# Layer 1's attention: queries and keys rounded ahead of the exponentials, and VectorE's slot put in another order

## The chip, the core and the metric

The kernel runs on one core of a Trainium2 chip. The metric is the device time of one execution in microseconds; several runs are taken and their median is given.

## What is computed

Two blocks of a gated cross-attention network on x of shape (8, 128, 512), each with a gated attention and a gated feed-forward part, all in float32:

```python
x = x + tanh(g_xattn[0]) * _L0_xattn_ref(_layernorm(x), ctx_4096, mask, ...)
x = x + tanh(g_ffn[0])   * _L0_ffn_ref(_layernorm(x), ...)
x = x + tanh(g_xattn[1]) * _L1_xattn_ref(_layernorm(x), ctx_4096, ...)
x = x + tanh(g_ffn[1])   * _L1_ffn_ref(_layernorm(x), ...)
```

The change concerns the third line. With 32 query heads that share 8 key/value heads, 128 queries a batch, and 256 keys (128 of the context, 128 of x itself):

```python
kv = concatenate([context, latents], axis=1)
q, k, v = latents @ Wq, kv @ Wk, kv @ Wv          # by head, 128 wide
q, k = rms_norm(q, q_norm_w), rms_norm(k, k_norm_w)
probs = softmax(q @ k.T / sqrt(128))
return (probs @ v, by head) @ Wo
```

## The kernel before, in words

There is no scheduler: each engine has its own instruction list, written by hand, and semaphores hold the lists together. The time up to about 940 us goes to layer 0 (keys and values of the context, attention, feed-forward). From there on layer 1's attention runs in 64 **slots**, the functions `slot1` of every engine. A slot is one key/value head and one batch; `BODY` = 8 slots (the batches) are a **turn**, and 8 turns are the heads. The first turn and the last are written out, those between are a loop.

Full precision is had from three passes of matmuls: every operand is split into a high part (the value rounded, by ScalarE, names in `_hi`) and a low part (what the rounding left, by VectorE, names in `_lo`), and `passes` multiplies high by high, high by low and low by high.

The work is pipelined over slots. In slot i, with count i + 1 as the current pair:

- **TensorE** (L2530 and on): keys and values of pair i + 2 (`keys_values`), transposes of q (L2547) and of k (L2552) for pair i + 1, the output projection of pair i - 2 (waits for `ot1_lo_done`), the queries of pair i + 2, the scores of pair i + 1 (wait for `qt1_lo_done`, `kt1_lo_done` and the earlier exponentials), and last the attention output of pair i - 1 (waits for `pt1_lo_done`).
- **ScalarE** (L1250 to L1285): `kv_out` (v_hi and the squares of k, L1213 and L1214), the four exponentials `exponentials1(i)` (L1235), qt_hi (L1263) and kt_hi (L1265), pt_hi (L1244, waits for the DMA that brings the transposed probabilities), in five slots a turn a piece of the next head's weights (`split_hi`, L1203), q_out (q_sb and q_sq, L1220 and L1221), and ot_hi (L1250, waits for the attention output).
- **VectorE** (L1974 to L2026): k_mean (k_ms, L1901), two reciprocals of the exponentials' sums (`inverse_sums1`, L1948), qt_lo (L1985), kt_lo (L1987), v_low (two v_lo, L1906), k_scaled (L1913, twice: the context's keys from SBUF, then x's own from a PSUM bank; its tile lies in `fbias`, and the rows call it so), `split_lo` (w_lo, L1896, in slots 1 to 5 of every turn but the last), accumulate1 (the residual, L1952), probabilities_lo (pt_lo, L1957), probabilities_in_blocks (two halves of 32x32 transposes, L1966), q_mean (q_ss and q_ms, L1920 and L1922), maxima1 (two nmax, L1938, and nb, L1943), output1_lo (ot_lo, L1971).
- **GpSimd**: k_root, `normalised(i)` (the probabilities times the reciprocals, two halves, L764, each behind its reciprocal), q_root (L630).
- **SP's queue**: the context's keys and values, the weights' pieces, and the round trip of the probabilities: a store to DRAM when both halves of blocks are made (L592), then four loads that bring them back transposed (L595) for pt_hi of the next slot.

The exponentials read the scores' banks, so the next scores wait for them; they wait for nb (`shift1_done`) and for the transposes of the pair before (`blocks1_done`), since these read the same tile p1.

Of the kernel before, what the change touches and what calls it, by code (L numbers as in the profile page):

```python
# [39 lines left out]
U = 64  # L40
# [17 lines left out]
def build(nc, x, ctx_t, mask, gates, wk0, wv0, wq0, w0, bias0, lnw, qweight, lut4, lut8, ffn0_bias, w1, qk_norm, ffn1_w, ffn1_bias, out):  # L58
    stack = ExitStack()
    with stack:  # L60
# [153 lines left out]
        sum1 = tmp("sum1", [P, 4], fp32)  # L214
        rn1 = tmp("rn1", [P, 4], fp32)
# [590 lines left out]
        def _(act):  # L806
# [424 lines left out]
            def exponentials1(count, parity):  # L1231
                act.wait_ge(shift1_done, count)
                wait(act, blocks1_done, 2 * (count - 1))
                for a in range(4):
                    last_op = nc.scalar.activation(p1[:, a, :], by2((S0B, S1B)[a // 2][:, :])[:, a % 2, :], ACT.Exp,  # L1235
                                                   bias=nb1[:, a:a + 1], scale=q_r[:, parity, a:a + 1],
                                                   accum_out=sum1[:, a:a + 1])
                    if a % 2:
                        last_op.then_inc(exp1_done, 1)
# [12 lines left out]
            def slot1(t, j):  # L1252
                i = BODY * t + j
                first = isinstance(t, int) and t == 0
                last = isinstance(t, int) and t == TL - 1

                if not (last and j == BODY - 1):
                    wait(act, o1_ps, i - 2)
                    kv_out(i + 2, (j + 1) % 4, 4 * t + (j + 1) // 2 + 1)
                if not (first and j == 0):  # L1260
                    exponentials1(i, (j - 1) % 2)
                act.wait_ge(qt1_ps, i + 1)
                nc.scalar.activation(qt_hi[:, :], QTB[:, :], ACT.Copy).then_inc(qt1_hi_done, 1)  # L1263
                act.wait_ge(kt1_ps, i + 1)
                nc.scalar.activation(kt_hi[:, :], KTB[:, 0:256], ACT.Copy, scale=kw[:, 0:1]).then_inc(kt1_hi_done, 1)  # L1265
                if first and j == 1:
                    transposed_hi(2, 6)
                    transposed_hi(2, 7)
# [47 lines left out]
        def _(dve):  # L1316
# [627 lines left out]

            def inverse_sums1(count):
                for half_p in (0, 2):
                    dve.wait_ge(exp1_done, 2 * count - 1 + half_p // 2)
                    nc.vector.reciprocal(rn1[:, half_p:half_p + 2], sum1[:, half_p:half_p + 2]).then_inc(recip1_done, 1)  # L1948

# [24 lines left out]
            def slot1(t, j):  # L1974
# [5 lines left out]
                if ahead:  # L1980
                    k_mean(i + 2)
                if lag1:
                    inverse_sums1(i)
                dve.wait_ge(qt1_hi_done, i + 1)
# [3 lines left out]
                                               in1=kt_hi[:, :].bitcast(fp32), op0=ALU.mult,  # L1988
                                               op1=ALU.subtract).then_inc(kt1_lo_done, 1)
                if ahead:  # L1990
                    v_low(i + 2, (j + 1) % 4)
                    k_scaled(i + 2, (j + 1) % 4)
                if not last and 1 <= j < 6:
                    split_lo(t + 1, j - 1, (t + 1) % 2)
                if not (first and j < 3):
                    accumulate1(i - 2, (j - 3) % B)
                if not (first and j < 2):
                    probabilities_lo(i - 1, (j - 1) % 2)
                if not (first and j < 1):
                    probabilities_in_blocks(i)  # L2000
                if last and j in (4, 6):
# [17 lines left out]
                if ahead:  # L2019
                    q_mean(i + 2)  # L2020
                maxima1(i + 1, j % 2)
                if first and j == 0:
                    transposed_lo(2, 4)
                    transposed_lo(2, 5)
                if not (first and j < 2):
                    output1_lo(i - 1)  # L2026
            for j in range(BODY):
                slot1(0, j)
# [7 lines left out]
            last_gate = tg[:, 3:4]  # L2036
            inverse_sums1(U)
            feed_forward(3, last_gate, 0)
# [627 lines left out]
```

## Time and profile before

| | |
|---|---|
| median of 3 runs | 1704.34 us (1704.33 to 1705.15) |
| the profiled execution | 1706.54 us |
| its span, first to last instruction | 1704.7 us |
| busy: TensorE matmuls / weight loads | 1643.4 (96%) / 1436.2 (84%) |
| busy: VectorE / ScalarE / GpSimd | 1230.3 (72%) / 1022.6 (60%) / 589.8 (35%) |
| granted TensorE clock, mean | 0.994 |
| layer 1's attention | from about 940 to 1690 us |

Busy shares are means over stages with different limits. To see what a slot waits for, the timeline of one slot is read engine by engine: a row gives the start and the duration of an instruction, and in brackets how long its engine stood idle before it and what ended that. Records of one engine overlap a little at their ends, so the distance of two starts is what an instruction costs its followers.

### The profile page before, as it was taken

What the parts mean: (1) busy time and instruction counts of PE and PEld (TensorE: products, weight loads), DVE (VectorE), ACT (ScalarE), POOL (GpSimd) and SP (SyncE); (2) the same over time, 40 slices, a digit from 0 to 9 for tenths busy, and PEclk for the clock granted to TensorE, in tenths of its full rate; (3) what the DMA queues carried; (4) which work ended last, traced back from release to release, by engine and by line L of the source; (5) the groups of instructions that cost most, each with busy time, mean ns of one, the idle gap of its engine ahead of it and who ended that gap; (6) DMA issues with size and microseconds to landing.
All of it is one profiled execution on the core that took longest, in us unless ns stands there. A gap on an engine that the chain in (4) does not pass through costs nothing.

```text
span 1704.7 us, 30549 instructions
## 1 busy us (share of the span) xinstructions
PE 1643.4 (96%) x9757; PEld 1436.2 (84%) x9757; DVE 1230.3 (72%) x2274; ACT 1022.6 (60%) x2511; POOL 589.8 (35%) x584
## 2 busy tenths in 40 slices
PE   9999999999999999999999799999999999999987
PEld 8899999999988888888888678888888888888875
DVE  6444437676787777877778677878787878777775
ACT  5344443345867677677766566666666666666652
POOL 3422223211334444444335333333333333333332
PEclk9999999999999999999999899999999999999999
DMA  6444444535233333333332243434343434343322
GB/s 231 171 166 148 148 171 157 191 133 182 72 106 102 120 98 111 113 95 126 98 106 82 72 136 122 148 119 146 118 159 123 145 123 148 123 148 111 115 93 97
DMA packets 126671, 220.43 MB, mean 129 GB/s; under 512 B 11664, under 2 KB 96016, under 8 KB 123024
## 3 DMA queue, kind: packets, MB, share of 16 engines
q1 hardware_dynamic: 126608, 219.63, 38.6%
q8 instruction: 35, 0.57, 0.1%
q14 instruction: 28, 0.23, 0.0%
HBM read 141.99 MB, written 77.59 MB: 129 GB/s over the span
## 4 chain that ended last, share of the span: by engine, by line
PE 58%; DVE 20%; ACT 9%; DMA 6%; issue 5%; SPq 1%; POOL 1%; DVEq 0%; ACTq 0%; POOLq 0%
PE bank L2134 20%; PE bank L2079 8%; PE bank L2080 8%; PE bank L2081 8%; PE bank L2311 6%; ACT p L1235 4%; DMA probabilities_transposed<-blocks_of_probabilities 2%; DMA blocks_of_probabilities<-probabilities_in_blocks 2%; DVE pt_lo L1957 2%; PE bank L2269 2%; PE bank L2347 2%; DVE probabilities_in_blocks L1966 2%; PE bank L2431 2%; DVE w_lo L1896 2%; DVE wl L1575 1%
## 5 line engine op out<-in xcount | busy, mean ns | idle before, releaser
L630 POOL TENSOR_TENSOR q_r<-q_ms,half 128x4 f32<-128x4 f32 x64 | 64.4, 1007 | 378.5 <-DVE q_ms L1922 378.5
L2079 PE MATMUL bank<-w_hi,xt_hi 128*128 (+2 forms) x512 | 173.4, 339 | 0.1
L2080 PE MATMUL bank<-w_lo,xt_hi 128*128 (+2 forms) x512 | 173.2, 338 | 0.0
L2081 PE MATMUL bank<-w_hi,xt_lo 128*128 (+2 forms) x512 | 172.0, 336 | 0.0
L711 POOL TENSOR_TENSOR pr<-pr,rn 128x512 f32<-128x512 f32 x64 | 67.5, 1055 | 291.4 <-DVE rn L1600 291.4
L1235 ACT ACTIVATE p<-bank,nb,q_r 128x256 f32<-128x256 f32 x256 | 141.4, 576 | 7.4 <-DVE nb L1943 7.4
L764 POOL TENSOR_TENSOR p<-p,rn 128x512 f32<-128x512 f32 x128 | 133.1, 1041 | 28.7 <-DVE rn L1948 25.2
L1244 ACT ACTIVATE pt_hi<-probabilities_transposed 128x1024 fp32r<-128x1024 f32 x64 | 68.0, 1063 | 94.6 <-DMA probabilities_transposed<-blocks_of_probabilities 94.6
L1075 ACT ACTIVATE pr<-sc,nmax 128x128 f32<-128x128 f32 x256 | 99.9, 391 | 40.0 <-DVE nmax L1585 39.6
L2079 PE MATMUL bank<-w_hi,ot_hi 128*128 (+1 forms) x256 | 107.3, 419 | 16.7 <-DVE ot_lo L1971 15.8
L2079 PE MATMUL bank<-w0o_hi,ot_hi 128*128 128x512 f32 x256 | 105.4, 412 | 5.0 <-DVE residual L1592 4.5
L1250 ACT ACTIVATE ot_hi<-bank 128x512 fp32r<-128x512 f32 x64 | 38.3, 598 | 119.2 <-PE bank L2081 119.2
L2079 PEld LDWEIGHTS bank<-w_hi,xt_hi 128*128 128x128 f32 x512 | 97.0, 189 | 13.9 <-POOL w_lo L728 0.3
L2080 PEld LDWEIGHTS bank<-w_lo,xt_hi 128*128 128x128 f32 x512 | 97.1, 190 | 12.0
L2081 PEld LDWEIGHTS bank<-w_hi,xt_lo 128*128 128x128 f32 x512 | 96.8, 189 | 10.9
L2134 PE MATMUL bank<-vw_hi,t_hi 128*128 128x256 f32 x368 | 104.1, 283 | 0.6 <-DVE vw_lo L1364 0.6
L2134 PE MATMUL bank<-vw_hi,t_lo 128*128 128x256 f32 x368 | 104.1, 283 | 0.0
L2134 PE MATMUL bank<-vw_lo,t_hi 128*128 128x256 f32 x368 | 104.1, 283 | 0.0
L1948 DVE RECIPROCAL rn<-sum 128x2 f32<-128x2 f32 x128 | 21.2, 166 | 110.9 <-ACT p L1235 110.9
L2080 PE MATMUL bank<-w_lo,ot_hi 128*128 (+1 forms) x256 | 101.1, 395 | 0.0
L2081 PE MATMUL bank<-w_hi,ot_lo 128*128 (+1 forms) x256 | 100.8, 394 | 0.0
L2081 PE MATMUL bank<-w0o_hi,ot_lo 128*128 128x512 f32 x256 | 100.1, 391 | 0.0
(292 smaller groups left out, 5574.6 us busy)
## 6 DMA issues: line engine op xcount, KB each, us to landing
blocks_of_probabilities<-probabilities_in_blocks SPq DMA_DIRECT2D x64, 512.0 KB, 2.7
probabilities_transposed<-blocks_of_probabilities SPq DMA_DIRECT2D x256, 128.0 KB, 2.8
stage<-w SPq DMA_DIRECT2D x35, 512.0 KB, 3.3
keys_of_layer<-kout SPq DMA_DIRECT2D x16, 1024.0 KB, 4.8
values_of_layer<-vout SPq DMA_DIRECT2D x16, 1024.0 KB, 5.2
kt<-keys_of_layer SPq DMA_DIRECT2D x64, 256.0 KB, 3.3
vs<-values_of_layer SPq DMA_DIRECT2D x64, 256.0 KB, 2.8
vraw<-wv SPq DMA_DIRECT2D x10, 1024.0 KB, 6.7
```

The source lines that it names most:

```text
L630: pool.tensor_tensor(dst, src, exponent, ALU.pow).then_inc(done, 1)
L711: pool.tensor_tensor(by4(pr), by4(pr), rn[:, :].unsqueeze(2).to_broadcast([P, 4, P]), ALU.mult).then_inc(norm_done, 1)
L764: pool.tensor_tensor(p1[:, half_p:half_p + 2, :], p1[:, half_p:half_p + 2, :], rn1[:, half_p:half_p + 2].unsqueeze(2).to_broadcast([P, 2, ...
L1075: last_op = nc.scalar.activation(by4(pr)[:, a, :], by4(sc)[:, a, :], ACT.Exp, bias=nmax[:, a:a + 1], accum_out=ssum[:, a:a + 1])
L1235: last_op = nc.scalar.activation(p1[:, a, :], by2((S0B, S1B)[a // 2][:, :])[:, a % 2, :], ACT.Exp, bias=nb1[:, a:a + 1], scale=q_r[:, pari ...
L1244: nc.scalar.activation(pt_hi[:, :, :].rearrange("p kc (qb n) -> p kc qb n", qb=4), by_key_block(ptr1[:, parity, :]), ACT.Copy).then_inc(pt ...
L1250: nc.scalar.activation(by_head(ot1_hi[:, :]), by_query_block(O1B[:, :]), ACT.Copy).then_inc(ot1_hi_done, 1)
L2079: nc.tensor.matmul(out_ap, l_hi, r_hi, start=(c == 0), stop=False)
L2080: nc.tensor.matmul(out_ap, l_hi, r_lo, start=False, stop=False)
L2081: op = nc.tensor.matmul(out_ap, l_lo, r_hi, start=False, stop=(c == n - 1))
L2134: op = nc.tensor.matmul(out_ap, l, r, start=start, stop=False, skip_group_check=True)
L2311: op = nc.tensor.matmul(bank[which][:, :], l[:, a, c, :], r[:, c, :], start=start, stop=False, skip_group_check=True)
```

## The change

On ScalarE, qt_hi and kt_hi move ahead of the exponentials. On VectorE the slot is reordered: the reciprocals, once together ahead of qt_lo, are taken apart; w_lo moves from behind k_scaled to between kt_lo and the first reciprocal; v_low stands between the two reciprocals and k_scaled behind the second; the transposes (probabilities_in_blocks) move ahead of pt_lo; and ot_lo moves ahead of the maxima. No instruction is added or removed; TensorE's, GpSimd's and SP's lists stay as they are.

```diff
--- before.py
+++ after.py
@@ -1257,12 +1257,12 @@
                 if not (last and j == BODY - 1):
                     wait(act, o1_ps, i - 2)
                     kv_out(i + 2, (j + 1) % 4, 4 * t + (j + 1) // 2 + 1)
-                if not (first and j == 0):
-                    exponentials1(i, (j - 1) % 2)
                 act.wait_ge(qt1_ps, i + 1)
                 nc.scalar.activation(qt_hi[:, :], QTB[:, :], ACT.Copy).then_inc(qt1_hi_done, 1)
                 act.wait_ge(kt1_ps, i + 1)
                 nc.scalar.activation(kt_hi[:, :], KTB[:, 0:256], ACT.Copy, scale=kw[:, 0:1]).then_inc(kt1_hi_done, 1)
+                if not (first and j == 0):
+                    exponentials1(i, (j - 1) % 2)
                 if first and j == 1:
                     transposed_hi(2, 6)
                     transposed_hi(2, 7)
@@ -1942,10 +1942,9 @@
                 dve.wait_ge(q1_root_done, count)
                 nc.vector.tensor_tensor(nb1[:, :], nmax1[:, :], q_r[:, parity, :], ALU.mult).then_inc(shift1_done, 1)
 
-            def inverse_sums1(count):
-                for half_p in (0, 2):
-                    dve.wait_ge(exp1_done, 2 * count - 1 + half_p // 2)
-                    nc.vector.reciprocal(rn1[:, half_p:half_p + 2], sum1[:, half_p:half_p + 2]).then_inc(recip1_done, 1)
+            def inverse_sums1(count, half_p):
+                dve.wait_ge(exp1_done, 2 * count - 1 + half_p // 2)
+                nc.vector.reciprocal(rn1[:, half_p:half_p + 2], sum1[:, half_p:half_p + 2]).then_inc(recip1_done, 1)
 
             def accumulate1(count, b):
                 dve.wait_ge(y1_ps, count)
@@ -1979,25 +1978,28 @@
                 ahead = not (last and j == BODY - 1)
                 if ahead:
                     k_mean(i + 2)
-                if lag1:
-                    inverse_sums1(i)
                 dve.wait_ge(qt1_hi_done, i + 1)
                 nc.vector.tensor_tensor(qt_lo[:, :], QTB[:, :], qt_hi[:, :].bitcast(fp32), ALU.subtract).then_inc(qt1_lo_done, 1)
                 dve.wait_ge(kt1_hi_done, i + 1)
                 nc.vector.scalar_tensor_tensor(out=kt_lo[:, :], in0=KTB[:, 0:256], scalar=kw[:, 0:1],
                                                in1=kt_hi[:, :].bitcast(fp32), op0=ALU.mult,
                                                op1=ALU.subtract).then_inc(kt1_lo_done, 1)
+                if not last and 1 <= j < 6:
+                    split_lo(t + 1, j - 1, (t + 1) % 2)
+                if lag1:
+                    inverse_sums1(i, 0)
                 if ahead:
                     v_low(i + 2, (j + 1) % 4)
+                if lag1:
+                    inverse_sums1(i, 2)
+                if ahead:
                     k_scaled(i + 2, (j + 1) % 4)
-                if not last and 1 <= j < 6:
-                    split_lo(t + 1, j - 1, (t + 1) % 2)
                 if not (first and j < 3):
                     accumulate1(i - 2, (j - 3) % B)
+                if lag1:
+                    probabilities_in_blocks(i)
                 if not (first and j < 2):
                     probabilities_lo(i - 1, (j - 1) % 2)
-                if not (first and j < 1):
-                    probabilities_in_blocks(i)
                 if last and j in (4, 6):
 
                     dve.wait_ge(acc1_done, i - 2)
@@ -2018,12 +2020,12 @@
                     transposed_lo(2, 7)
                 if ahead:
                     q_mean(i + 2)
+                if not (first and j < 2):
+                    output1_lo(i - 1)
                 maxima1(i + 1, j % 2)
                 if first and j == 0:
                     transposed_lo(2, 4)
                     transposed_lo(2, 5)
-                if not (first and j < 2):
-                    output1_lo(i - 1)
             for j in range(BODY):
                 slot1(0, j)
             with dve.Fori(1, TL - 1) as t:
@@ -2034,7 +2036,8 @@
 
 
             last_gate = tg[:, 3:4]
-            inverse_sums1(U)
+            inverse_sums1(U, 0)
+            inverse_sums1(U, 2)
             feed_forward(3, last_gate, 0)
             transposed_lo(3, 1)
             probabilities_in_blocks(U)
```

ScalarE, a slot without a weight's piece (the names: p is the exponentials' output). Before:

```order
L1214 ACTIVATE fbias,k_ss<-bank 128x128
L1235 ACTIVATE p,sum<-bank,nb,q_r 128x256 x4
L1263 ACTIVATE qt_hi<-bank 128x512
L1265 ACTIVATE kt_hi<-bank,kw 128x256
L1244 ACTIVATE pt_hi<-probabilities_transposed 128x1024
L1220 ACTIVATE q_sb<-bank 128x512
```

Now:

```order
L1214 ACTIVATE fbias,k_ss<-bank 128x128
L1261 ACTIVATE qt_hi<-bank 128x512
L1263 ACTIVATE kt_hi<-bank,kw 128x256
L1235 ACTIVATE p,sum<-bank,nb,q_r 128x256 x4
L1244 ACTIVATE pt_hi<-probabilities_transposed 128x1024
L1220 ACTIVATE q_sb<-bank 128x512
```

qt_hi and kt_hi have passed the four exponentials; pt_hi follows these directly.

VectorE, one slot of the first turn with a weight's piece, from the ot_lo that closes the slot before to pt_lo (fbias is k_scaled's tile). Before:

```order
L1971 TENSOR_TENSOR ot_lo<-bank,ot_hi 128x512
L1901 TENSOR_SCALAR k_ms<-k_ss 128x2
L1948 RECIPROCAL rn<-sum 128x2 x2
L1985 TENSOR_TENSOR qt_lo<-bank,qt_hi 128x512
L1987 SCALAR_TENSOR_TENSOR kt_lo<-bank,kw,kt_hi 128x256
L1906 TENSOR_TENSOR v_lo<-keys_values_of_context,v_hi 128x128
L1906 TENSOR_TENSOR v_lo<-bank,v_hi 128x128
L1913 TENSOR_SCALAR fbias<-keys_values_of_context,k_r 128x128
L1913 TENSOR_SCALAR fbias<-bank,k_r 128x128
L1896 TENSOR_TENSOR w_lo<-stage,w_hi 128x1024
L1952 SCALAR_TENSOR_TENSOR residual<-bank,tg,residual 128x512
L1957 TENSOR_TENSOR pt_lo<-probabilities_transposed,pt_hi 128x1024
```

Now, the same stretch from its ot_lo to the first k_scaled:

```order
L1970 TENSOR_TENSOR ot_lo<-bank,ot_hi 128x512
L1938 TENSOR_REDUCE nmax<-bank 128x2 x2
L1943 TENSOR_TENSOR nb<-nmax,q_r 128x4
L1901 TENSOR_SCALAR k_ms<-k_ss 128x2
L1982 TENSOR_TENSOR qt_lo<-bank,qt_hi 128x512
L1984 SCALAR_TENSOR_TENSOR kt_lo<-bank,kw,kt_hi 128x256
L1896 TENSOR_TENSOR w_lo<-stage,w_hi 128x1024
L1947 RECIPROCAL rn<-sum 128x2
L1906 TENSOR_TENSOR v_lo<-keys_values_of_context,v_hi 128x128
L1906 TENSOR_TENSOR v_lo<-bank,v_hi 128x128
L1947 RECIPROCAL rn<-sum 128x2
L1913 TENSOR_SCALAR fbias<-keys_values_of_context,k_r 128x128
```

Before, both reciprocals stand ahead of qt_lo, and w_lo behind k_scaled; the maxima and nb are ahead of this ot_lo, outside the rows. Now the maxima and nb follow ot_lo, w_lo stands ahead of the first reciprocal, v_lo behind the first and k_scaled behind the second. The end of the slot, now:

```order
L1913 TENSOR_SCALAR fbias<-bank,k_r 128x128
L1951 SCALAR_TENSOR_TENSOR residual<-bank,tg,residual 128x512
L1965 STREAM_TRANSPOSE probabilities_in_blocks<-p 128x2x2x4x32 x2
L1956 TENSOR_TENSOR pt_lo<-probabilities_transposed,pt_hi 128x1024
L1920 TENSOR_REDUCE q_ss<-q_sq 128x4
```

The transposes stand ahead of pt_lo, and behind q_ss and q_ms the next ot_lo follows directly.

## Rows read from the trace of the kernel before

**Rows 1.** Waits, TensorE's weight loads, 1010 to 1650 us: total us, times, longest.
```profile
PEld bank L2079 <- DVE ot_lo L1971: 19.5, 38, 2.1
PEld bank L2079 <- DVE pt_lo L1957: 12.8, 34, 1.5
```

**Rows 2.** Timeline, ScalarE, 1326 to 1339 us: start, duration, engine, line, operation [idle before].
```profile
1326.80 0.60 ACT L1250 ACTIVATE ot_hi<-bank 128x512 fp32r<-128x512 f32 x1 [2.54 <-PE bank L2081]
...
1328.64 0.57 ACT L1235 ACTIVATE p<-bank,nb,q_r 128x256 f32<-128x256 f32 x1
...
1330.81 0.62 ACT L1263 ACTIVATE qt_hi<-bank 128x512 fp32r<-128x512 f32 x1
1331.28 0.51 ACT L1265 ACTIVATE kt_hi<-bank,kw 128x256 fp32r<-128x256 f32 x1
...
1338.07 0.60 ACT L1250 ACTIVATE ot_hi<-bank 128x512 fp32r<-128x512 f32 x1 [1.70 <-PE bank L2081]
```

**Rows 3.** Timeline, ScalarE, 1371 to 1405 us.
```profile
1371.86 0.60 ACT L1250 ACTIVATE ot_hi<-bank 128x512 fp32r<-128x512 f32 x1 [2.12 <-PE bank L2081]
...
1404.26 0.60 ACT L1250 ACTIVATE ot_hi<-bank 128x512 fp32r<-128x512 f32 x1 [1.50 <-PE bank L2081]
```

**Rows 4.** Timeline, VectorE, 1326 to 1339 us.
```profile
1326.95 1.29 DVE L1938 TENSOR_REDUCE nmax<-bank 128x2 f32<-128x512 f32 x2
1328.28 0.16 DVE L1943 TENSOR_TENSOR nb<-nmax,q_r 128x4 f32<-128x4 f32 x1
1328.36 0.68 DVE L1971 TENSOR_TENSOR ot_lo<-bank,ot_hi 128x512 fp32r<-128x512 f32 x1
...
1329.88 0.17 DVE L1948 RECIPROCAL rn<-sum 128x2 f32<-128x2 f32 x1 [0.76 <-ACT p L1235]
...
1331.46 0.69 DVE L1985 TENSOR_TENSOR qt_lo<-bank,qt_hi 128x512 fp32r<-128x512 f32 x1 [0.32 <-ACT qt_hi L1263]
1332.07 0.47 DVE L1987 SCALAR_TENSOR_TENSOR kt_lo<-bank,kw,kt_hi 128x256 fp32r<-128x256 f32 x1
...
1332.86 0.28 DVE L1913 TENSOR_SCALAR fbias<-keys_values_of_context,k_r 128x128 f32<-128x128 f32 x1
...
1333.32 1.22 DVE L1896 TENSOR_TENSOR w_lo<-stage,w_hi 128x1024 f32 x1
1334.45 0.75 DVE L1952 SCALAR_TENSOR_TENSOR residual<-bank,tg,residual 128x512 f32<-128x512 f32 x1
1335.11 1.22 DVE L1957 TENSOR_TENSOR pt_lo<-probabilities_transposed,pt_hi 128x1024 fp32r<-128x1024 f32 x1
1336.24 1.30 DVE L1966 STREAM_TRANSPOSE probabilities_in_blocks<-p 128x512 f32<-128x512 f32 x2
1337.46 0.64 DVE L1920 TENSOR_REDUCE q_ss<-q_sq 128x4 f32<-128x512 f32 x1
```

**Rows 5.** Timeline, GpSimd, 1329 to 1333 us.
```profile
1330.12 2.13 POOL L764 TENSOR_TENSOR p<-p,rn 128x512 f32<-128x512 f32 x2 [0.23 <-DVE rn L1948]
```

**Rows 6.** Timeline, VectorE and GpSimd side by side, at 499 and 933 us.
```profile
499.53 1.87 DVE L1616 TENSOR_TENSOR w0o_lo<-stage0o,w0o_hi 128x1024 fp32r<-128x1024 f32 x1
...
499.14 1.17 POOL L689 TENSOR_TENSOR bm<-bias_sb,negm 128x512 f32<-128x512 f32 x1
500.27 1.71 POOL L659 TENSOR_TENSOR qraw<-qraw 128x256 f32<-128x256 f32 x1
...
933.70 4.77 POOL L728 TENSOR_TENSOR w_lo<-plain,w_hi 128x1024 fp32r<-128x1024 f32 x2
...
936.76 1.73 DVE L1337 TENSOR_SCALAR base_b<-mv 128x2 f32<-128x2 f32 x1
```

**Rows 7.** Timeline, VectorE and ScalarE, three late waits of layer 1.
```profile
1001.47 1.23 DVE L1957 TENSOR_TENSOR pt_lo<-probabilities_transposed,pt_hi 128x1024 fp32r<-128x1024 f32 x1 [1.47 <-ACT pt_hi L1244]
...
1591.10 1.23 DVE L1957 TENSOR_TENSOR pt_lo<-probabilities_transposed,pt_hi 128x1024 fp32r<-128x1024 f32 x1 [2.16 <-ACT pt_hi L1244]
...
1629.83 0.56 ACT L1235 ACTIVATE p<-bank,nb,q_r 128x256 f32<-128x256 f32 x1 [1.26 <-DVE nb L1943]
```

## The prediction

> **What bounds the kernel now.** I read the waits of TensorE first, then the rhythm of one ScalarE instruction, then one slot instruction by instruction on VectorE and ScalarE, and last GpSimd beside VectorE. The change touches layer 1's attention alone: 64 slots, eight to a turn, and only there TensorE's order meets VectorE's. In [rows 1] the weight loads of TensorE stand idle 19.5 us for ot_lo (the low part of the attention output, wanted by the output projection) and 12.8 us for pt_lo (the low part of the transposed probabilities, wanted by the attention output). Some 30 us is thus all that a better order could win.
>
> The rhythm is the start of ot_hi on ScalarE, once a slot. From 1326.80 to 1338.07 [rows 2] is 11.27 us, and the three slots from there to 1371.86 [rows 3] take 11.26 each: these are slots in which VectorE also makes a weight's low part, w_lo. Those without it, 1371.86 to 1404.26 [rows 3], take 32.40 for three, 10.80 each. Per turn five slots have w_lo (35 in all, the last turn has none) and three have not (21 in turns 0 to 6).
>
> Why 11.27: a loop closes on itself in every slot. ot_hi starts at 0 (1326.80), the exponentials at 1.84, qt_hi at 4.01, kt_hi at 4.48 [rows 2]; VectorE then runs without a gap qt_lo, kt_lo, the v and k operations, w_lo, the residual, pt_lo [rows 4]; pt_lo releases the attention output, and that the next ot_hi. pt_lo starts at 1335.11 and ot_hi at 1338.07, so **pt_lo to ot_hi is 2.96**. The 2.17 us of exponentials ahead of qt_hi lie in this loop, and VectorE mostly waits under them (the reciprocal of 1329.88 was 0.76 us idle before, [rows 4]). TensorE and VectorE are both nearly full, the loop is what is too long.
>
> **The change, part by part.** Steps on VectorE are distances of starts in [rows 4]: nmax to nb 1.33, nb to ot_lo 0.08 (I take 0.08 for each tiny operation: nb, k_ms, a reciprocal), qt_lo to kt_lo 0.61 (ot_lo, of the same shape, taken as 0.60), kt_lo 0.39 (its 0.47 less the overlap of 0.08 that its neighbours show), the two v_lo 0.40 (kt_lo to k_scaled, 0.79, less the 0.39), the two k_scaled 0.46, w_lo 1.13, residual 0.66, pt_lo 1.13, the pair of transposes 1.22. An activation of 128x512 to its follower is 0.65 (qt_hi 1330.81 to qt_lo 1331.46).
>
> *With w_lo*, from ot_hi at 0. ot_lo now stands ahead of the maxima, and starts at 0.65; maxima 1.25; nb 2.58; k_ms 2.66; qt_lo 2.74. qt_hi has taken the exponentials' place at 1.84, so its result was there at 2.49: no wait. kt_lo 3.35, w_lo 3.74, first reciprocal 4.87, v_lo 4.95, second reciprocal 5.35, k_scaled 5.43. The exponentials start at 2.80 (1.84, then 0.47 for qt_hi and 0.49 for kt_hi, its 0.51 less a little overlap), just behind nb's end at 2.74. The first reciprocal of before started 1.24 behind their start [rows 2, 4]; that gives 4.04, and the second, half of 2.17 later, 5.13: neither holds VectorE here.
>
> Now GpSimd. It normalises in two halves, the first 0.24 behind its reciprocal's start (1329.88 to 1330.12, [rows 4, 5]), at 5.11. The pair took 2.13 with the second half held 1.09 by its reciprocal, so a half is 1.04. **In the kernel before no k_scaled runs beside it** (the pair ends at 1332.25, k_scaled starts at 1332.86); in the changed one it comes due at 5.43, in the middle of the first half. What that costs I read from other stages [rows 6]. w0o_lo, two SBUF inputs and w_lo's shape, took 1.87 for 1.22 when it was issued 0.39 into a GpSimd addition of 1.17; it got going 1.05 after the addition's start, 0.12 ahead of its recorded end. GpSimd's next operation, already due at 500.27, took 1.71 in its turn: the waiting VectorE operation went first. And base_b, a tensor_scalar of two columns with SBUF on both sides, took 1.73 beside GpSimd. k_scaled's first tile is a tensor_scalar from SBUF to SBUF, so I let it wait until 5.11 + 1.04 - 0.12 = 6.03. The rest follows: residual 6.49, transposes 7.15, pt_lo 8.37, next ot_hi 11.33. **That is 0.07 more than 11.26**, though 2.17 us of exponentials have left the chain: ot_lo, the maxima, the transposes and this wait have come into it. 35 x 0.07 = **+2.4 us**. Free of the wait k_scaled starts at 5.43; the normalising then decides the second transpose (second half ends 7.19), pt_lo 7.85, slot 10.81. Both ends of the unknown price, 0 and 0.60, go into the range; I take 0.60 by the row of the same kind of instruction.
>
> The Trainium skill, "SBUF — State Buffer", section "SBUF: two separate sides", says that VectorE operations in a two-port mode or with two SBUF inputs and GpSimd share a port pair as an exclusive lock for the whole instruction. By its word k_scaled would wait to the half's recorded end, 6.15, a slot of 11.45; the rows show 0.12 less. This is the rule that speaks against the change.
>
> *Without w_lo.* The reciprocals wait for the exponentials: 4.04 and 5.13. GpSimd starts at 4.28 and lets go at 5.20; k_scaled comes due at 5.21, just behind. Residual 5.67, transposes 6.33; the second half runs 5.37 to 6.41 and the second transpose at 6.94 finds it done; pt_lo 7.55, slot **10.51**. 21 x (10.80 - 10.51) = **-6.1 us**.
>
> *Output projection.* ot_lo ends 1.34 behind ot_hi's start; before, it started at 1.56 (1326.80 to 1328.36). So the 19.5 us of [rows 1] go. They are not a further gain: TensorE then waits for pt_lo instead, since the slot's length is the loop's.
>
> *Round trip.* The transposes stood behind pt_lo, now ahead of it; at 7.15 or 6.33 behind ot_hi instead of 9.44 (1336.24, [rows 2, 4]); the store to DRAM and the four loads on SP's queue start as much earlier. Long landings that held pt_lo should vanish: the 1.47 us at 1001.47, and that of 1591.10, 2.16 idle, in a slot without w_lo (priced 1.9) [rows 7]. **-1.5 and -1.9**.
>
> *Last turn.* It has the layer norm's statistics in VectorE's queue; nb came 1.26 us late for the exponentials at 1629.83 [rows 7]. Transposes and pt_lo stand ahead of them as before, ot_lo goes first after: I take **-1.3**, and 2 x 0.3 = **-0.6** for two more plain slots.
>
> Moved at no cost: the exponentials (their buffers are read by the transposes, which wait for GpSimd anyway), w_lo (its stage is then free 2 us sooner, a weight's load hangs on that), q_mean (the q copy ends behind the queries' matmuls, as before). No DMA is added, and no instruction.
>
> Sum: +2.4 - 6.1 - 1.5 - 1.9 - 1.3 - 0.6 = **-9.0 us**. The profiled execution took 1706.54 (span 1704.7), 2.2 above the median of 1704.34, so 1697.5 on its scale and **1695.3** on the median's.
>
> **Rivals.**
> (a) *k_scaled doesn't wait.* Nothing in the trace shows this very instruction beside GpSimd; base_b is a near kin. Then 35 x (11.33 - 10.81) = 18.2 less: **1677.1**.
> (b) *Slower: k_scaled waits for both halves.* GpSimd's second half is due 0.12 us behind the first one's release, and might win the pair again; k_scaled then starts 1.04 later, every slot with w_lo with it: +36.4, **1731.7**. It decides as soon as k_scaled starts later than 6.29 instead of 6.03 (9.0 / 35 = 0.26). Against it: [rows 6], where the waiting VectorE operation passed GpSimd's next one.
> (c) *The wait lasts to the half's recorded end*, a lock on GpSimd's whole instruction: 35 x 0.12 = 4.2 more, **1699.5**. The Trainium skill's rule named above would give this one; base_b and w0o_lo speak for the shorter wait.
> (d) *No change:* the new order frees nothing, since another of VectorE's waits fills it (k_scaled for its root, or nb late for the exponentials, where my margin is only 0.06): about **1703**. The plain slots alone give 6 us, and all 21 would have to fail.
>
> **How the numbers follow.** Forecast 0.58, (a) 0.17, (b) 0.08, (c) 0.10, (d) 0.07. The likeliest gives 1695.3. The range goes from just below (a), 1676, to 1701, behind (c); outside are (b) and (d). 0.2% is 3.4 us, about what a measurement of this kernel can tell. Faster: forecast, (a), and most of (c), 0.80; same: (d) and the tail of (c), 0.11; slower: (b) and a bit more, 0.09.
>
> **What would show it.** In the profile after, with ot_hi's start as zero: ot_lo at 0.65 and no TensorE wait for it; the first k_scaled with a record of some 0.9 us instead of 0.28 in slots with w_lo, and of 0.28 in the others; slots of 11.3 and 10.5; TensorE's waits all on pt_lo. A k_scaled of 0.28 everywhere and slots of 10.8 mean (a); one of 1.9 means (b). pt_hi should start right behind the exponentials. I am wrong as a whole if ot_lo is late again, or if the exponentials wait for nb.

## The result, and the profile after

| | before | after |
|---|---|---|
| median, us (lowest to highest, 4 runs each) | 1704.34 (1704.03 to 1705.15) | **1684.84** (1683.03 to 1686.66) |
| ratio, 95% interval | | 0.9885 (0.9868 to 0.9902) |
| the profiled execution, us | 1706.54 | 1683.03 |
| its span, us | 1704.7 | 1681.2 |
| busy TensorE matmuls / VectorE / ScalarE, us | 1643.4 / 1230.3 / 1022.6 | 1625.6 / 1240.0 / 1026.7 |
| granted clock, mean | 0.994 | 0.998 |

The kernel is faster by 19.5 us, where 9.0 were forecast. The sign and the wait on GpSimd came as predicted; 10.5 us of the gain, more than half, were not in the sum.

The waits of layer 1 after, 1010 to 1640 us (engine and line waited for: us in total, times, longest), answer to [rows 1]:

```profile
DVE ot_lo L1970 <- ACT ot_hi L1250: 85.3, 56, 1.6
PEld bank L2082 <- DVE pt_lo L1956: 24.9, 31, 1.6
PE bank L2082 <- DVE pt_lo L1956: 18.7, 31, 1.4
```

TensorE's wait for ot_lo is gone but for one of 1.0 us (before, 19.0 in this window), and those for pt_lo grew from 12.8 to 24.9 (the PE and the PEld row are one wait, seen at the matmul and at its weights' load). VectorE now idles 1.6 us in a slot, ahead of ot_lo.

ScalarE after, 1312 to 1325 us (start, duration, engine, line, operation, in brackets the idle time before it), and the ot_hi of the slots without w_lo; it answers to [rows 2, 3]:

```profile
1312.83 0.60 ACT L1250 ACTIVATE ot_hi<-bank 128x512 fp32r<-128x512 f32 x1 [2.55 <-PE bank L2084]
...
1314.68 0.60 ACT L1261 ACTIVATE qt_hi<-bank 128x512 fp32r<-128x512 f32 x1
...
1315.66 0.57 ACT L1235 ACTIVATE p<-bank,nb,q_r 128x256 f32<-128x256 f32 x1
...
1317.85 1.07 ACT L1244 ACTIVATE pt_hi<-probabilities_transposed 128x1024 fp32r<-128x1024 f32 x1
...
1324.03 0.60 ACT L1250 ACTIVATE ot_hi<-bank 128x512 fp32r<-128x512 f32 x1 [2.56 <-PE bank L2084]
...
1357.64 0.60 ACT L1250 ACTIVATE ot_hi<-bank 128x512 fp32r<-128x512 f32 x1 [2.61 <-PE bank L2084]
...
1389.12 0.60 ACT L1250 ACTIVATE ot_hi<-bank 128x512 fp32r<-128x512 f32 x1 [1.82 <-PE bank L2084]
```

A slot with w_lo is 11.20 us long (before 11.26), one without 10.49 (31.48 for three; before 10.80). pt_hi follows the exponentials without a gap.

VectorE in the same slot, and GpSimd's normalising beside it; they answer to [rows 4, 5]:

```profile
1313.46 0.69 DVE L1970 TENSOR_TENSOR ot_lo<-bank,ot_hi 128x512 fp32r<-128x512 f32 x1 [1.60 <-ACT ot_hi L1250]
...
1315.56 0.69 DVE L1982 TENSOR_TENSOR qt_lo<-bank,qt_hi 128x512 fp32r<-128x512 f32 x1
...
1316.56 1.22 DVE L1896 TENSOR_TENSOR w_lo<-stage,w_hi 128x1024 f32 x1
...
1318.22 0.83 DVE L1913 TENSOR_SCALAR fbias<-keys_values_of_context,k_r 128x128 f32<-128x128 f32 x1
1318.97 0.34 DVE L1913 TENSOR_SCALAR fbias<-bank,k_r 128x128 f32<-128x128 f32 x1
1319.23 0.73 DVE L1951 SCALAR_TENSOR_TENSOR residual<-bank,tg,residual 128x512 f32<-128x512 f32 x1
1319.89 1.29 DVE L1965 STREAM_TRANSPOSE probabilities_in_blocks<-p 128x512 f32<-128x512 f32 x2
1321.11 1.18 DVE L1956 TENSOR_TENSOR pt_lo<-probabilities_transposed,pt_hi 128x1024 fp32r<-128x1024 f32 x1
```
```profile
1317.93 2.04 POOL L764 TENSOR_TENSOR p<-p,rn 128x512 f32<-128x512 f32 x2 [1.49 <-DVE rn L1947]
```

The first k_scaled is 0.83 us long instead of 0.28: it came 0.29 into GpSimd's first half. Its follower starts 0.75 later, where an undisturbed one starts 0.19 later (1325.33 to 1325.52, first experiment): **it was held 0.56 us**, of 0.60 forecast. It came through at about 1318.78, 0.85 behind the half's start.

The other place is the start of layer 1. First ScalarE and TensorE before (TensorE's row is its scores), then the same after:

```profile
969.43 0.56 ACT L1235 ACTIVATE p<-bank,nb,q_r 128x256 f32<-128x256 f32 x1 [2.80 <-DVE nb L1943]
...
971.61 0.60 ACT L1263 ACTIVATE qt_hi<-bank 128x512 fp32r<-128x512 f32 x1
...
973.40 0.19 PEld L2079 LDWEIGHTS bank<-kt_hi,qt_hi 128*128 128x128 f32 x1 [4.35 <-DVE qt_lo L1985]
...
979.53 0.60 ACT L1250 ACTIVATE ot_hi<-bank 128x512 fp32r<-128x512 f32 x1 [2.66 <-PE bank L2081]
```
```profile
964.53 0.60 ACT L1261 ACTIVATE qt_hi<-bank 128x512 fp32r<-128x512 f32 x1
...
966.26 0.56 ACT L1235 ACTIVATE p<-bank,nb,q_r 128x256 f32<-128x256 f32 x1 [0.77 <-DVE nb L1943]
...
968.67 0.19 PEld L2082 LDWEIGHTS bank<-kt_hi,qt_hi 128*128 128x128 f32 x1 [1.62 <-issue]
...
974.26 0.60 ACT L1250 ACTIVATE ot_hi<-bank 128x512 fp32r<-128x512 f32 x1 [1.27 <-PE bank L2084]
```

In the first slots nb is late for the exponentials. Before, qt_hi and so the next scores stood behind that wait, and TensorE idled 4.35 us there and 1.23 more ahead of ot_hi; after, qt_hi is done ahead of it and TensorE idles 1.62 and 2.42. Of the 5.27 us between the two first ot_hi, 1.4 is the executions' own (the z_mid of 946.95 in one starts at 945.51 in the other, before anything that the change touches). So **some 3.8 us come from the start** in these two executions, and none of it was in the sum. Four more profiles show the same stretch, from z_mid to the first ot_hi: that of experiment 12 with the old order there, and those of experiments 11, 1 and 2 with the new one (1 and 2 differ from after only behind the third slot, so not ahead of the first ot_hi).

| | before | run 12 | after | run 11 | run 1 | run 2 |
|---|---|---|---|---|---|---|
| z_mid to first ot_hi, us | 32.58 | 32.62 | 28.75 | 28.65 | 30.07 | 30.85 |
| of it, TensorE not busy | 7.64 | 6.93 | 6.24 | 6.19 | 6.12 | 6.20 |
| granted clock | 0.81 | 0.79 | 0.94 | 0.94 | 0.89 | 0.85 |

Every stretch with the new order is shorter, but by 1.7 to 4.0 us. TensorE idles 0.7 to 1.5 less in it, and the granted clock was higher in all four, though not by the same amount. No run changes the clock by itself, so how much of the gain is its doing stays open.

### The profile page after: what moved, and what is told of

Read it like the earlier page. It is cut to its first block, busy times and chain, and to the rows that moved or that the text cites. A ratio compares the mean times of both kernels' runs of the same rounds, so it can differ in the third digit from the quotient of the medians.

```text
span 1681.2 us, 30543 instructions
## 1 busy us (share of the span) xinstructions
PE 1625.6 (97%) x9757; PEld 1431.4 (85%) x9757; DVE 1240.0 (74%) x2274; ACT 1026.7 (61%) x2511; POOL 588.2 (35%) x584
## 4 chain that ended last, share of the span: by engine, by line
PE 65%; DVE 23%; issue 5%; ACT 5%; DMA 1%; POOL 0%; DVEq 0%; SPq 0%; ACTq 0%
PE bank L2137 22%; PE bank L2082 10%; PE bank L2084 9%; PE bank L2083 9%; PE bank L2314 6%; DVE nmax L1938 3%; DVE probabilities_in_blocks L1965 3%; DVE pt_lo L1956 2%; DVE w_lo L1896 2%; PE bank L2272 2%; PE bank L2350 2%; PE bank L2434 2%; DVE residual L1951 2%; DVE fbias L1913 1%; ACT ot_hi L1250 1%
## 5 line engine op out<-in xcount | busy, mean ns | idle before, releaser
L1970 DVE TENSOR_TENSOR ot_lo<-bank,ot_hi 128x512 fp32r<-128x512 f32 x64 | 44.3, 692 | 94.7 <-ACT ot_hi L1250 94.7
L630 POOL TENSOR_TENSOR k_r<-k_ms,half 128x2 f32<-128x2 f32 x64 | 44.7, 699 | 164.8 <-DVE k_ms L1901 164.8
L2083 PE MATMUL bank<-w0o_lo,ot_hi 128*128 128x512 f32 x256 | 100.0, 391 | 0.0
```

The source lines that it names most:

```text
L630: pool.tensor_tensor(dst, src, exponent, ALU.pow).then_inc(done, 1)
L2083: nc.tensor.matmul(out_ap, l_hi, r_lo, start=False, stop=False)
```

## Experiments

Each is the changed kernel with one thing altered; the diffs show VectorE's slot unless they say otherwise. Each was timed in three rounds against the kernel before on the same chip (its medians there were 1704.38, 1701.63 and 1704.95 us), so the ratios carry the comparison.

**1. The residual ahead of k_scaled in slots with w_lo.**

```diff
-                if ahead:
-                    k_scaled(i + 2, (j + 1) % 4)
                 if not (first and j < 3):
                     accumulate1(i - 2, (j - 3) % B)
+                if ahead:
+                    k_scaled(i + 2, (j + 1) % 4)
```

> The changed kernel with one swap, in the slots that have w_lo only: the residual stands ahead of the two k_scaled. Theory L (k_scaled's first tile waits for GpSimd's normalising of the first half, 0.55 us in each of these slots, and the wait lies in the slot's loop): the residual, which has an operand in PSUM, runs beside GpSimd at its 0.73 us, k_scaled comes due when the half is done and its record falls from 0.82 to 0.28 us; slots with w_lo go from 11.20 to about 10.65; 35 x 0.55 = 19 us, 1666 us. Rival W (the 11.20 come from w_lo's own 1.13 us on a full VectorE, and the long record covers other waiting): no change, 1685 us.

Measured 1675.35 us (1671.99 to 1675.95), ratio 0.9819 (0.9791 to 0.9846). The timeline of VectorE:

```profile
1324.68 0.73 DVE L1951 SCALAR_TENSOR_TENSOR residual<-bank,tg,residual 128x512 f32<-128x512 f32 x1
1325.33 0.27 DVE L1913 TENSOR_SCALAR fbias<-keys_values_of_context,k_r 128x128 f32<-128x128 f32 x1
1325.52 0.34 DVE L1913 TENSOR_SCALAR fbias<-bank,k_r 128x128 f32<-128x128 f32 x1
1325.78 1.46 DVE L1965 STREAM_TRANSPOSE probabilities_in_blocks<-p 128x512 f32<-128x512 f32 x2
```

k_scaled is back at 0.27; the residual, which has moved ahead of it, reads a PSUM bank and passes beside GpSimd undelayed. The gain is 9 us short of what was expected, since the slot is 10.81 us, not 10.65: the second transpose now waits for GpSimd's second half (the pair is 1.46 instead of 1.29). The wait on GpSimd costs about 35 x 0.39 = 13.7 us by these slots, and 11 by the two ratios (0.0066 of 1704); its price is thus 0.3 to 0.4 us a slot, less than the 0.56 of the hold.

**2. The residual ahead of k_scaled in every slot.** The same edit without the condition on the slot.

> The residual stands ahead of k_scaled in every slot, not only in those with w_lo as in the earlier run of 1675. Theory (k_scaled waits only where it comes due inside a GpSimd half): in the slots without w_lo it now comes due inside the second half and is held some 0.4 us, those slots grow from 10.49 to about 10.9, and the time is about 1684 us. Rival (the hold-up is a matter of the slots with w_lo alone): plain slots stay at 10.49, 1675 us.

Measured 1683.51 us (1681.34 to 1685.55), ratio 0.9874 (0.9856 to 0.9892), as expected. In a slot without w_lo, VectorE and GpSimd:

```profile
1373.75 0.64 DVE L1913 TENSOR_SCALAR fbias<-keys_values_of_context,k_r 128x128 f32<-128x128 f32 x1
1374.31 0.34 DVE L1913 TENSOR_SCALAR fbias<-bank,k_r 128x128 f32<-128x128 f32 x1
```
```profile
1372.17 2.13 POOL L764 TENSOR_TENSOR p<-p,rn 128x512 f32<-128x512 f32 x2 [0.71 <-DVE rn L1947]
```

There k_scaled now falls into the second half, is held 0.37, and the slot grows from 10.49 to 10.85. The same instruction waits or not by where it falls, as the theory had it.

**3. w_lo back behind k_scaled.**

```diff
-                if not last and 1 <= j < 6:
-                    split_lo(t + 1, j - 1, (t + 1) % 2)
                 if lag1:
                     inverse_sums1(i, 0)
...
                     k_scaled(i + 2, (j + 1) % 4)
+                if not last and 1 <= j < 6:
+                    split_lo(t + 1, j - 1, (t + 1) % 2)
```

> The weights' low part goes back behind k_scaled (and ahead of the residual); everything else stays as in the changed kernel, so this is the place of w_lo alone. Theory (w_lo, with two SBUF inputs and one SBUF output, waits for a GpSimd half as k_scaled does): k_scaled comes due about 1.13 us earlier and the second GpSimd half then runs over the start of w_lo, which waits for it: w_lo 1.9 us long by its record or more, slots with it near 12.1, about 1717 us. Rival (w_lo waits for nothing, or only for the first half): slots with it near 11.2 to 11.6, 1685 to 1699 us.

Measured 1722.93 us (1721.71 to 1723.78), ratio 1.0107 (1.0090 to 1.0125): **slower than the kernel before**, by 1.1%. Slots with w_lo are 12.25 us (12.1 and 1717 us were expected). VectorE and GpSimd:

```profile
1342.50 0.27 DVE L1913 TENSOR_SCALAR fbias<-keys_values_of_context,k_r 128x128 f32<-128x128 f32 x1
...
1342.94 1.84 DVE L1896 TENSOR_TENSOR w_lo<-stage,w_hi 128x1024 f32 x1
```
```profile
1341.57 2.13 POOL L764 TENSOR_TENSOR p<-p,rn 128x512 f32<-128x512 f32 x2 [0.71 <-DVE rn L1947]
```

k_scaled slips into the gap between the halves; w_lo, 0.28 into the second half, takes 1.84 for 1.22, in all 35 slots. And since the reciprocals no longer have w_lo ahead of them, VectorE also waits 0.25 and 0.54 us for the exponentials' sums. So w_lo at its old place loses twice, by its own wait and by the idle time that it leaves: 38 us between the two medians, all the gain of the other moves and more. k_scaled itself is not held at 1342.50, though the first half, 1.04 long, is recorded until 1342.61.

**4. w_lo behind q_ms.** There VectorE idles for ot_hi.

> The changed kernel with w_lo moved out of the loop: from ahead of the first reciprocal to behind q_ms, where VectorE stands idle 1.6 us for ot_hi. Theory L: slots with w_lo become like the plain ones, 10.5 instead of 11.20 us, since k_scaled then comes due behind GpSimd's first half and w_lo's 1.13 us fill idle time; 35 x 0.7 = 24 us, 1660 us. GpSimd's q root starts about 1 us later, unseen. Rival W: VectorE has the same work, so nothing is gained, 1685 us.

Measured 1808.99 us (1805.39 to 1810.64), ratio 1.0610 (1.0581 to 1.0639). Expected was a gain. SP's queue and ScalarE show why:

```profile
1312.54 0.36 SPq L585 DMA_DIRECT2D stage<-w  x1
1313.01 0.37 SPq L592 DMA_DIRECT2D blocks_of_probabilities<-probabilities_in_blocks  x1
1317.97 1.75 SPq L595 DMA_DIRECT2D probabilities_transposed<-blocks_of_probabilities  x4
```
```profile
1322.61 1.06 ACT L1244 ACTIVATE pt_hi<-probabilities_transposed 128x1024 fp32r<-128x1024 f32 x1 [4.74 <-DMA probabilities_transposed<-blocks_of_probabilities]
```

On SP the weight's next piece (L585) stands ahead of the round trip's store (L592) and waits for w_lo (here at 1311.15, 1.23 long), whose buffer it fills. With w_lo behind q_ms the store waits for it too, and ScalarE idles 4.74 us for the landing. The slots with w_lo are mostly 12.9 to 16.8 us long; part of that goes with the granted clock, which was 0.81 to 0.85 in the whole of several of them (0.81 in the one of 16.66 us from 1115.47) and 1.00 in the slots without w_lo.

**5. The same, and on SP the round trip ahead of the piece.** SP's slot:

```diff
+                if not (static and t == 0 and j < 1):
+                    probabilities_round_trip(BODY * t + j, j % 4)
                 if piece is not None:
                     sp.wait_ge(w1_lo_done[read_before], t + 1)
...
-                if not (static and t == 0 and j < 1):
-                    probabilities_round_trip(BODY * t + j, j % 4)
```

> w_lo behind q_ms as in the run that took 1809 us, and on SP's queue the round trip of the probabilities ahead of the weight's next piece. Theory Q (there the store of the probabilities stood in SP's queue behind a wait for that slot's w_lo, so pt_hi came 4 to 5 us late; w_lo itself costs nothing in the idle time of VectorE): slots with w_lo 10.5 us, 1660 us. Rival W (w_lo's 1.13 us must be paid wherever it stands): 1685 us or more.

Measured **1661.46 us** (1660.52 to 1662.38), ratio 0.9759 (0.9743 to 0.9776): the fastest of these. In the six middle turns every slot, with w_lo or without, takes 10.48 to 10.54 us. TensorE's weight loads there, 1010 to 1640 us:

```profile
PEld bank L2082 <- DVE pt_lo L1956: 4.2, 2, 2.6
```

Of the 24.9 us for pt_lo 4.2 are left: TensorE is the bound in nearly every slot (busy 10.50 of 10.50 us from 1333.62 to 1344.12). Yet experiments 7 and 8 have slots of 10.39 with the same list on TensorE; these 0.1 us weren't traced. The price of w_lo's place shows on GpSimd:

```profile
1343.30 1.98 POOL L630 TENSOR_TENSOR q_r<-q_ms,half 128x4 f32<-128x4 f32 x1 [3.22 <-DVE q_ms L1922]
```

q_r takes 1.98 us beside w_lo (1343.19, 1.23 long) and 1.01 elsewhere. Here it is VectorE that holds GpSimd, and the slots, no longer than those without w_lo, show no cost of it.

**6. The order on SP alone.** The diff of 5 on the changed kernel, w_lo in its place.

> The changed kernel with SP's queue alone reordered: the probabilities' round trip ahead of the weight's piece. Theory (there w_lo is done before the transposes, so the queue isn't held): no change, 1685 us. Rival (the store of the probabilities is delayed by the piece's issue too, and the landing counts): a slot is shorter by 0.1 us or more, 1680 us or less.

Measured 1684.73 us (1683.93 to 1686.74), ratio 0.9890 (0.9872 to 0.9907), no change from the changed kernel, as expected. The 22 us between 5 and this run (0.0131 of 1704) thus belong to w_lo's place, and the queue's order only makes it possible.

**7. ot_lo behind the maxima again.**

```diff
-                if not (first and j < 2):
-                    output1_lo(i - 1)
                 maxima1(i + 1, j % 2)
...
+                if not (first and j < 2):
+                    output1_lo(i - 1)
```

> The changed kernel with one part undone: ot_lo behind the maxima and nb again. Theory L: ScalarE's qt_hi and not ot_lo is then what the slot's first part waits for; the maxima run while VectorE waits for ot_hi, ot_lo starts hardly later, qt_lo at 2.5 instead of 2.74: slots with w_lo 0.2 us shorter, plain ones the same: 1678 us. Rival O (ot_lo's place is what took TensorE's 19.5 us of waiting away): these waits come back, about 0.3 us a slot, 1695 to 1700 us.

Measured 1674.54 us (1673.5 to 1676.36), ratio 0.9816 (0.9791 to 0.9842). VectorE:

```profile
1343.22 1.29 DVE L1938 TENSOR_REDUCE nmax<-bank 128x2 f32<-128x512 f32 x2
...
1344.88 0.69 DVE L1970 TENSOR_TENSOR ot_lo<-bank,ot_hi 128x512 fp32r<-128x512 f32 x1 [0.18 <-ACT ot_hi L1250]
1346.23 0.17 DVE L1901 TENSOR_SCALAR k_ms<-k_ss 128x2 f32<-128x2 f32 x1 [0.66 <-ACT fbias L1214]
```

The maxima need no ot_hi and fill the idle time ahead of it, and ot_lo still starts 0.63 behind ot_hi (1344.25). Slots with w_lo are 10.96 us, those without 10.39. This move of the change costs 10 to 12 us (by the medians, and by the ratios). Without it TensorE's 19.5 us for ot_lo [rows 1] are gone as well (3.4 us are left, in two waits), since in the shorter chain ot_hi starts 1.03 behind the maxima and no longer 0.15 ahead of them.

**8. Both 5 and 7.**

> The best version so far (1661.5 us: w_lo behind q_ms, SP's round trip ahead of the weight's piece), and ot_lo behind the maxima again as in the kernel before. Theory (ot_lo needn't go first, and its move costs some 0.1 us in a slot without w_lo): slots near 10.39, 1656 us. Rival (with w_lo now ahead of the maxima, nb or ot_lo comes late and the gain is gone): 1661 us or more.

Measured 1681.43 us (1680.87 to 1682.37), ratio 0.9867 (0.9850 to 0.9884): the rival, and 20 us slower than 5. Slots with w_lo are 11.05 to 11.22, the others 10.39. w_lo and the maxima use the same idle time. VectorE and TensorE, one slot:

```profile
1346.09 1.23 DVE L1896 TENSOR_TENSOR w_lo<-stage,w_hi 128x1024 f32 x1
1347.23 1.28 DVE L1938 TENSOR_REDUCE nmax<-bank 128x2 f32<-128x512 f32 x2
...
1348.63 0.68 DVE L1970 TENSOR_TENSOR ot_lo<-bank,ot_hi 128x512 fp32r<-128x512 f32 x1
```
```profile
1349.37 0.19 PEld L2082 LDWEIGHTS bank<-w_hi,ot_hi 128*128 128x128 f32 x1 [0.64 <-DVE ot_lo L1970]
```

**9. The transposes behind pt_lo again.**

```diff
-                if lag1:
-                    probabilities_in_blocks(i)
                 if not (first and j < 2):
                     probabilities_lo(i - 1, (j - 1) % 2)
+                if lag1:
+                    probabilities_in_blocks(i)
```

> The changed kernel with one part undone: the transposes stand behind pt_lo again. Theory L (the loop from pt_lo over the attention output, ot_hi, ot_lo to the next pt_lo sets the slot): 1.22 us leave that loop, but the round trip of the probabilities then closes a loop of its own (pt_lo, transposes 2.4 us, landing 7.0, pt_hi 1.06: 10.5 us): slots 10.5 to 10.7 with and without w_lo, 1666 us. Rival R (the gain of the change came from the earlier round trip): the late landings come back, pt_lo waits for pt_hi in most slots, 1690 us or more.

Measured 1677.06 us (1676.85 to 1678.24), ratio 0.9833 (0.9807 to 0.9858). Expected were 1666 us, by the rival 1690 or more; it lies between. Its slots swing between 10.4 and 11.1 in most of the loop. One is 13.73: it is the slot that begins with the 55th ot_hi, and pt_lo waits 3.25 us for a late landing in it, as it did in the kernel before (2.16 at 1591.10). VectorE and ScalarE:

```profile
1316.78 1.23 DVE L1956 TENSOR_TENSOR pt_lo<-probabilities_transposed,pt_hi 128x1024 fp32r<-128x1024 f32 x1 [0.68 <-ACT pt_hi L1244]
```
```profile
1315.69 1.06 ACT L1244 ACTIVATE pt_hi<-probabilities_transposed 128x1024 fp32r<-128x1024 f32 x1 [1.60 <-DMA probabilities_transposed<-blocks_of_probabilities]
```

Now the landing is late, and yet this beats the change by 8 us: 1.22 us of transposes leave the chain, 0.68 of waiting comes in. In the loop the move costs time; what it buys is slots that are all alike, and 10.42 for 13.73 where the landing is late.

**10. The exponentials ahead of qt_hi and kt_hi again.** ScalarE's part of the change undone, VectorE's kept.

> The changed kernel with ScalarE's order undone: the exponentials ahead of qt_hi and kt_hi again, VectorE's order as changed. Theory L (one loop per slot): qt_lo starts at 4.66 behind ot_hi instead of 2.74, with w_lo, the reciprocals, the transposes and pt_lo all behind it; slots of 13.1 us with w_lo and 12.0 without; 35 x 1.9 + 29 x 1.5 = 110 us, 1795 us: slower than the kernel before by far. Rival F (ScalarE's order gives about what it frees, VectorE's the rest): about half of the gain is left, 1695 us.

Measured 1890.01 us (1889.19 to 1891.62), ratio 1.1104 (1.1086 to 1.1123). The slots are 13.0 to 15.5 us, and the time is 95 us over the theory's 1795. From 1010 us on TensorE's weight loads wait 134.9 us for pt_lo, and VectorE:

```profile
DVE qt_lo L1982 <- ACT qt_hi L1263: 128.7, 48, 2.8
```

With ot_lo ahead of the maxima the exponentials wait for nb, qt_hi for the exponentials, qt_lo for qt_hi: all in one line. The two halves of the change need each other. Two things that the theory left out stand in the rows. k_scaled is 0.82 or 0.83 long in 62 of the 64 slots, in those without w_lo too. And the granted clock is lower: of the slots from 1012 to 1368 us those with w_lo are 14.1 to 14.5 us long at 0.97 to 1.00, and 14.9 to 15.5 at 0.83 to 0.86. Why they are 14.1 and not 13.1 at the full clock was not traced.

**11 and 12. The change in the first turn only, and in the last only.** The slots of the other turns have the old order on ScalarE and VectorE.

> The change in the first turn alone (slots 0 to 7); all other slots are those of the kernel before. Theory S (the first slots gain more than the 1.5 us that the prediction gave them, since in the profile after the first seven ot_hi of layer 1 come 6.4 to 7.9 us sooner): 1704.3 - 7.9 = 1696.4 us. Rival N (the difference in the two profiles is mostly the scatter of single executions; only the late landing of 1001.47 is gained): 1702.5 us.

Measured 1697.93 us (1694.93 to 1700.08, 10 runs), ratio 0.9977 (0.9967 to 0.9987).

> The change in the last turn alone (slots 56 to 63 and the tail), all others as before. Theory S (all six intervals between the ot_hi of this turn fall to 10.4 us, 5.8 us together in the profiles): 1698.6 us. Rival P (the 3.8 us of the prediction): 1700.5 us.

Measured 1696.96 us (1694.98 to 1700.23, 8 runs), ratio 0.9972 (0.9962 to 0.9983). The first turn gives 3.9 us (2.2 to 5.6); theory had 7.9 and the rival 1.8, and neither lies in the interval. The last gives 4.8 (2.9 to 6.5), which doesn't decide between the theory's 5.8 and the rival's 3.8. That leaves some 11 of the 19.5 for the six between (7 to 15, the three intervals together). The rows show 7 there: from the 7th to the 55th ot_hi it is 524.94 us after, 531.65 in run 11 and 532.23 in run 12. So the rows reach only the lower end of what the times leave for these turns.

## Why the prediction was too small

The order of the waits in a slot, the hold of k_scaled and the slots without w_lo came as predicted. Two steps failed. The term of +2.4 us for the slots with w_lo was mis-sized: it measured -2.1. And the start of layer 1 had no term at all: it gave 1.7 to 4.0 us. Beside these, the terms of the last turn were too small.

Distances of ot_hi, counted from the first one of layer 1 and summed by eight, in us (the last turn begins with the 55th; "run 11" and "run 12" are the experiments with the change in the first and in the last turn only):

| | 1 to 8 | 9 to 16 | each eight to 48 | 49 to 56 | 57 to 63 |
|---|---|---|---|---|---|
| before | 91.53 | 89.74 | 88.60 to 88.73 | 89.56 | 82.78 |
| old order there | 88.64 (run 12) | 89.10 (run 11) | 88.45 to 88.62 (run 11) | 88.99 (run 11) | 81.76 (run 11) |
| after | 87.24 | 87.53 | 87.50 | 85.83 | 78.61 |

*Slots without w_lo.* Forecast 10.51, measured 10.49, first k_scaled undisturbed (durations of 0.27 there). All 21 together are 6.0 us shorter than in run 12 (226.1 to 220.2), of -6.1 forecast. **Right.**

*Slots with w_lo.* **The first step that failed:** the forecast's +2.4 was mis-sized. The order, the wait and its kind were right: k_scaled at 5.39 behind ot_hi (5.43), pt_lo at 8.28 (8.37), the slot 11.20 instead of 11.33. Of the 0.13, 0.08 come from k_scaled, due 0.04 sooner and held 0.04 less, the rest from pt_lo to ot_hi, 2.92 for 2.96, and from rounding. Times 35 it is 4.6 us, and turns +2.4 into **-2.1** (the 33 that lie behind the first ot_hi take 369.6 us, 2.5 less than in run 12; the other two lie ahead of it). A sum of some fifteen steps was compared with 11.26 and multiplied by 35; its error was as large as half the forecast.

*The start.* **The second step that failed:** from the rows of the steady loop I priced nothing ahead of the first ot_hi. The wait of 2.80 for nb at 969.43 was there in the trace of before, with qt_hi behind it. It gave 3.8 us in the profiled execution, 1.7 to 4.0 over the six profiles; a part of it comes with a higher granted clock, which the forecast didn't consider either.

*Round trip.* The 1.47 us at 1001.47 did go, but it seems to be that execution's own: in run 12, with the old order in turn 0, none of the first six slots is over 11.26. The slot of 1591.10 was 12.39 long, came again in run 11 (12.01) and is 10.42 now: 1.6 to 2.0, so the term of -1.9 was real. Experiment 9, with the transposes behind pt_lo, has the wait again.

*Last turn.* The term of -1.3 for the late nb came, and was too small. The slot of 1629.83 was 12.54 long (12.41 in run 11, where the exponentials waited 1.13 for nb) and is 10.44 now, 2.0 to 2.1 less. In the same slot of after nb starts at 1608.27 and the exponentials follow without a wait. They still wait two slots later, in a slot whose like before had such a wait too (1.54, at 1652.62) and wasn't priced:

```profile
1608.47 0.59 ACT L1235 ACTIVATE p<-bank,nb,q_r 128x256 f32<-128x256 f32 x1
...
1630.38 0.57 ACT L1235 ACTIVATE p<-bank,nb,q_r 128x256 f32<-128x256 f32 x1 [1.83 <-DVE nb L1943]
```

The layer norm's statistics stand behind pt_lo and ahead of the maxima in both orders. What has changed is that the transposes no longer stand between pt_lo and them: before, the statistics started 0.66 ahead of ot_hi (1625.88 to 1626.54), now 1.82 ahead of it (1603.89 to 1605.71). From the 55th ot_hi to the last it is 99.43 us after and 104.68 in run 11: 5.2 us, of 3.8 forecast.

Together, against the table's second row: start -3.8, then -1.4, -1.6, -4.0, -3.2 and -3.1, in all **-17.1**, or 15.0 to 17.3 with the start's range. The measured ratio allows 16.7 to 22.5, so the rows reach its lower end, and some 2 to 4 of the 19.5 us are placed in no slot. Single executions differ by as much: ahead of layer 1, where all have like code, z_mid starts between 945.5 and 947.9 in the fourteen profiles.

*The rivals.* (a), no wait, gives 1677.1 and slots of 10.81; the wait is there, and experiment 1, which takes it away, measured 1675.35 and 10.81. (b), a wait for both halves, would be a record of 1.9 us; it isn't. (c), to the half's recorded end: the half starts at 1317.93 and is about 1.04 long, so its end is near 1318.97, and k_scaled came through at about 1318.78, some 0.2 sooner (the profile's spans on GpSimd are rough). Here lies the rule of the Trainium skill, "SBUF — State Buffer", section "SBUF: two separate sides", by which the two engines exclude each other for the whole instruction; the runs agree on which instructions wait, and put the release earlier than the recorded end. (d), no change, would have been 1703.

## What to carry to other kernels

When two engines' order is changed, price the first and the last rounds from their own rows, not only the steady loop: here a wait that the loop hides, that for nb, was bare where the pipeline fills. A slot's length that results from a long sum of steps was off by 0.13 us here, so multiply such an error by the count before trusting a small difference. And before moving an instruction into a neighbour's idle time, ask who waits for its result in another queue: w_lo cost 124 us or won 22 at the same place, by the order of two transfers on SP.

## What the runs showed of the hardware

- A tensor_scalar of 128 columns from SBUF to SBUF and a 1024-column subtraction with two SBUF inputs both wait while a GpSimd tensor_tensor is under way (0.83 and 0.64 for 0.27; 1.84 for 1.22). Issued 0.11 ahead of the half's recorded end k_scaled was not held (0.27 at 1342.50, experiment 3). Instructions of VectorE that read a PSUM bank beside it did not wait (the residual, 0.73 in both places), and v_lo from SBUF, two inputs of 128 columns, was 0.28 when it was issued just ahead of the half.
- The one that waits goes in between GpSimd's two: after, the second half was due from 1318.39 (the second reciprocal at 1318.15 and 0.24), k_scaled came through at 1318.78, and the two halves still took 2.04 together. It works the other way as well: q_r on GpSimd took 1.98 for 1.01 beside w_lo.
- A store to DRAM that followed a weight's piece on the same queue took 4.96 us from its issue to that of the loads that wait for it (1313.01 to 1317.97, experiment 4), and 2.68 without one just ahead (1341.31 to 1343.99, experiment 5).
- The granted clock at the start of layer 1 (stretch, busy time of PE, PEld, DVE, ACT and POOL, then the clock, the DMA share and GB/s), before and after:

```profile
970.00:980.00 10.00, 5.61 (x22) 4.79 (x23) 7.85 (x17) 6.02 (x14) 3.33 (x4) 0.72 0.54 170
```
```profile
970.00:980.00 10.00, 7.76 (x46) 6.61 (x44) 8.31 (x18) 8.43 (x22) 2.99 (x4) 1.00 0.47 161
```

Before, the clock was at the lower of its two levels (1.2 of 2.4 GHz) from 976 to 980 us, granted 0.50, behind TensorE's idle 4.35 us; after, it stayed at 1.00. Run 11, with the new order, had 1.00 there and run 12, with the old one, 0.57. Yet experiments 1 and 2, with idle times as short as after's, had 0.80 and 0.65, so the idle time alone does not tell. As an estimate, length times what the clock lacks of 1.00 is, from z_mid to the first ot_hi, 6.2 and 6.8 us in the two profiles with the old order and 1.7 to 4.6 in the four with the new one.
